# Routing tokens to experts: places counted one group later, five row buffers, a written-out group loop, and one expert tile fewer

## The reference, cut to what matters

```python
xn = layernorm(x)
h  = tanh(mean_by_dst(xn[src]) @ W1_l.T + xn @ W1_r.T + b1)
g  = mean_by_dst(h[src]) @ W2_l.T + h @ W2_r.T + b2
x2 = x + g + linear_attention(xn)          # 8 heads, q/k feature maps elu(..)+1
xf = layernorm(x2)
logits = xf @ Wr + br                       # 8 experts
e, gate = top_1(softmax over the one kept)  # gate is exp(0)/exp(0)
out = x2 + gate * (relu(xf @ W1[e] + b1[e]) @ W2[e] + b2[e])
```

## Time and profile before

| | |
|---|---|
| median of 3 runs | 2648.65 us (2645.68 to 2650.23) |
| profiled execution | 2644.86 us, its span 2642.9 us |
| TensorE busy over the span | 2436.1 us (92%) |
| VectorE, ScalarE, GpSimd busy | 1777.5, 1116.8, 1186.0 us |
| TensorE clock granted, mean | 0.967 of full |
| DMA | 511.55 MB, mean 194 GB/s |
| routing, table and empty rows, expert tiles | from about 2126, 2356 and 2374 us of the span |

### The profile page before, as it was taken

One profiled execution on the slowest core, in us unless ns is written; L12 is line 12 of the kernel. 1 busy time (PEld: TensorE's weight loads), 2 busy tenths in 40 slices (PEclk: granted clock), 3 DMA queues, 4 the chain that ended last, 5 costly groups with the idle time before them and its releaser, 6 DMA issues.

```text
span 2642.9 us, 39517 instructions
## 1 busy us (share of the span) xinstructions
PE 2436.1 (92%) x11512; PEld 1931.0 (73%) x11513; DVE 1777.5 (67%) x3701; ACT 1116.8 (42%) x2055; POOL 1186.0 (45%) x1092
## 2 busy tenths in 40 slices
PE   5999999999999998999999899899999957759897
PEld 4788888888888886888888566677777745547675
DVE  5677777767877763444344477788878567747887
ACT  3455455444444443444334323233333245535554
POOL 5576777666666660000000045555555435542333
PEclk8999999999999999999999999999999979879999
DMA  9866656455555545544444467788888687745554
GB/s 371 250 174 187 195 159 190 120 151 142 125 149 129 140 115 185 224 170 168 188 191 176 153 190 212 219 233 240 228 226 237 157 345 292 280 144 185 182 180 140
DMA packets 159400, 511.55 MB, mean 194 GB/s; under 512 B 30354, under 2 KB 30866, under 8 KB 126658
## 3 DMA queue, kind: packets, MB, share of 16 engines
q1 hardware_dynamic: 110020, 381.71, 40.8%
q0 software_dynamic: 49280, 128.61, 22.1%
HBM read 268.06 MB, written 244.32 MB: 194 GB/s over the span
## 4 chain that ended last, share of the span: by engine, by line
PE 80%; DMA 8%; DVE 5%; issue 3%; POOL 2%; ACT 1%; SPq 1%; DVEq 0%; POOLq 0%; ACTq 0%
PE bank L1363 53%; PE bank L1414 8%; PE bank L1370 5%; DMA agg_d<-O,eidx 4%; PE bank L1614 4%; PE bank L1478 2%; PE bank L1547 1%; PE bank L453 1%; PE bank L454 1%; PE bank L1617 1%; POOL r_rows L809 1%; DMA a_x<-in_x 1%; DVE r_rows L1227 1%; DVE pd L1192 1%; DVE st L1230 1%
## 5 line engine op out<-in xcount | busy, mean ns | idle before, releaser
L414 POOL DMA_INDIRECT agg_d<-O,eidx x160 | 274.4, 1715 | 221.2 <-DMA agg_d<-O,eidx 163.2
L350 POOL TENSOR_TENSOR G_low<-G,G_high 128x512 fp32r<-128x512 f32 x160 | 237.9, 1487 | 227.9 <-ACT G_high L475 227.5
L397 POOL DMA_INDIRECT G<-y_d,esrc x80 | 85.2, 1065 | 527.2 <-DMA y_d<-b_y 514.3
L433 DVE SCALAR_TENSOR_TENSOR Sj<-erow,dstf,tri 128x128 f32<-128x128 int32 x160 | 190.1, 1188 | 30.7 <-DMA agg_d<-O,eidx 30.6
L475 ACT CAST G_high<-G 128x512 fp32r<-128x512 f32 x160 | 99.2, 620 | 180.7 <-DVE G L1077 172.8
L820 POOL DMA_INDIRECT out<-x_out,x_id x88 | 84.4, 959 | 188.8 <-DVE x_out L1318 184.7
L442 DVE SCALAR_TENSOR_TENSOR eidx<-cnt,todump,dstf 128x1 int32<-128x1 f32 x160 | 149.1, 932 | 7.6
L948 ACT CAST qz_high<-low 128x512 fp32r<-128x512 f32 x80 | 49.6, 620 | 235.2 <-PE bank L1363 135.6
L774 POOL TENSOR_TENSOR pd<-pd,low 128x512 f32<-128x512 f32 (+1 forms) x80 | 142.1, 1776 | 0.0
L350 POOL TENSOR_TENSOR a_xn_rows_low<-a_x,a_xn_rows_high 128x512 fp32r<-128x512 f32 x80 | 141.6, 1771 | 0.3 <-ACT a_xn_rows_high L846 0.3
L1363 PE MATMUL bank<-Wk_high,xnT_high 128*128 128x512 f32 x320 | 127.8, 399 | 6.3 <-DVE xnT_low L350 6.3
(11 more groups left out here) (227 smaller groups left out, 7512.9 us busy)
## 6 DMA issues: line engine op xcount, KB each, us to landing
x_rows<-xs_d SPq DMA_DIRECT2D x88, 260.0 KB, 2.7
agg_d<-zero SPq DMA_DIRECT2D x20, 1040.0 KB, 20.2
b_agg<-agg_d SPq DMA_DIRECT2D x20, 1040.0 KB, 8.8
a_x<-in_x SPq DMA_DIRECT2D x20, 1024.0 KB, 7.3
agg_d<-z_halves SPq DMA_DIRECT2D x20, 1024.0 KB, 5.9
q_d<-q_rows SPq DMA_DIRECT2D x80, 256.0 KB, 2.4
r_d<-r_rows SPq DMA_DIRECT2D x80, 256.0 KB, 3.8
r_in<-r_d SPq DMA_DIRECT2D x20, 1024.0 KB, 6.8
```

Source lines behind the costliest of these rows:

```text
L350: return eng.tensor_tensor(out_, full, high.bitcast(F32), ALU.subtract)
L397: pool.indirect_dma_start(G[:, j, :], None, table, bass.IndirectOffsetOnAxis(ap=esrc[:, b, j:j + 1], axis=0)).then_inc(e_g[j], 16)
L414: pool.indirect_dma_start(agg, bass.IndirectOffsetOnAxis(ap=eidx[:, j, 0:1], axis=0), O[:, j, 0:width], None, compute_op=ALU.add).then_inc ...
L433: dve.scalar_tensor_tensor(Sj[:, :], row, dstf[:, b, j:j + 1], tri[:, :], ALU.is_equal, ALU.mult, accum_out=cnt[:, j:j + 1]).then_inc(e_cn ...
```

## The change

- `places()` is done one step later, for group g-3 at the start of VectorE's step g. VectorE's order becomes places, x2(0), x2(1), x2(2), best, x2(3). The scatter of GpSimd keeps its step.
- TensorE's `rank()` stands behind `logits(1)` instead of ahead of it.
- `r_rows`, the places and the scatter semaphores get five buffers (`RING`). The fifth takes the room of `r_part` buffer 1, which moves to the tile `G` of the edge stage, and of the copied logits, which move to `low`. SyncE waits for the last reader of `G`.
- `group_steps` writes all steps out on all five engines: no hardware loop, and waits on constants.
- The empty rows are loaded once into SBUF (`x_pad`, at step 17) and written from there.
- The 2 MB load of `W1x` moves from SyncE's step 3 to step 17. VectorE's copy into `W1x` (L1284 before) moves to the end of the table.
- `XT` is 87: the 8 experts can leave at most 8 x 127 rows unfilled, so 87 tiles hold all rows.

Cut to its core:

```diff
-XT = NT + EXP
+XT = (NP + EXP * (P - 1)) // P
+RING = 5
-def quad_turns(eng, body, tail, last=0):
-    for k in range(4):
-        body(0, k)
-    with eng.Fori(1, NG // 4 - last) as it:
-        for k in range(4):
-            body(it, k)
-...
+def group_steps(body, tail):
+    for g in range(NG + tail):
+        body(g)
...
-        rp = [at(f"r_part{i}", s, shape=[P, TG, D]) for i, s in enumerate((18, 10, 11, 14))]
+        rp = [at(f"r_part{i}", s, shape=[P, TG, D]) for i, s in ((0, 18), (2, 11), (3, 14))]
-        rows = at("r_rows", 5, shape=[P, 4, TG, AW])
+        rows = at("r_rows", 5, shape=[P, RING, TG, AW])
-        lgT = at("r_logitsT", 9.125, shape=[P, 2, GROUP])
+        pad = at("x_pad", 10.125, shape=[P, AW])
+        rp, lgT = [rp[0], G, *rp[1:]], low
...
             part_in(3, 3)
+            sp.wait_ge(e_gl, 2 * NT)
             sp.wait_ge(m_st[0], 16 * PAIRS)
...
-                if isinstance(g, int) and g == 3:
+                if g == 17:
+                    sp.dma_start(pad[:, :], pad_in).then_inc(r_pad, 16)
                     for n in range(2):
                         sp.dma_start(W1x[:, TG * D * n:TG * D * (n + 1)].bitcast(F32),
                                      f1_d[n][:]).then_inc(s_f, 16)
...
-                sp.dma_start(xs_d[bass.ds(end, P), :], pad_in).then_inc(r_pad, 16)
+                sp.dma_start(xs_d[bass.ds(end, P), :], pad[:, :]).then_inc(r_pad, 16)
...
@@ vector @@
-                        need(dve, r_sc[k], 64 * turn)
+                        need(dve, r_sc[k], 64 * (g // RING))
...
+                if g == 2:
+                    dve.wait_ge(m_st[0], 16 * PAIRS)
+                    dve.memset(rows[:, 4:RING, :, D:AW], 0.0)
+                if active(g, 3, NG):
+                    places()
                 x2(0)
                 x2(1)
+                x2(2)
                 if active(g, 2, NG):
                     best()
-                x2(2)
-                if active(g, 2, NG):
-                    places()
                 x2(3)
-            quad_turns(dve, route, 2)
+            group_steps(route, 3)
...
@@ tensor @@
                     turn_row(2)
+                    logits(1)
                 if active(g, 2, NG):
                     rank()
                 if active(g, 1, NG):
-                    logits(1)
                     turn_row(3)
```

More of the change, by code:

```diff
@@ L309, in build @@
         r_in = [sem(f"r_part_and_agg_in{k}") for k in range(4)]
-        r_sc = [sem(f"r_scattered{k}") for k in range(4)]
+        r_sc = [sem(f"r_scattered{k}") for k in range(RING)]
         r_x2 = sem("r_rdegree_x2_stats")
@@ L694, in _, with route @@
                 agg_in(k, k)
[L697 to L700, removed]
+            def route(g):
+                k = g % 4
+                if g >= 4:
+                    sp.wait_ge(r_x2, 13 * (g - 3) - 2)
                     part_in(g, k)
                     agg_in(g, k)
-                if isinstance(g, int) and g == 3:
+                if g == 17:
+                    sp.dma_start(pad[:, :], pad_in).then_inc(r_pad, 16)
                     for n in range(2):
@@ L706, in route @@
                                      f1_d[n][:]).then_inc(s_f, 16)
-                if isinstance(g, int) and g == 16:
+                if g == 16:
                     for twice in range(2):
@@ L710, in route @@
                             w2_in(W2a, twice, odd, f2_d[0])
-            quad_turns(sp, route, 0, last=1)
+            group_steps(route, 0)
+            sp.wait_ge(r_pad, 16)
             sp.wait_ge(r_tb, 1)
@@ L716, in _ @@
                 end = sp.value_load(runi[0:1, e:e + 1], min_val=0, max_val=EXP * REG - P)
-                sp.dma_start(xs_d[bass.ds(end, P), :], pad_in).then_inc(r_pad, 16)
-            for k in range(4):
-                sp.wait_ge(r_sc[k], 16 * NT // 4)
-            sp.wait_ge(r_pad, 16 * EXP)
+                sp.dma_start(xs_d[bass.ds(end, P), :], pad[:, :]).then_inc(r_pad, 16)
+            for k in range(RING):
+                sp.wait_ge(r_sc[k], 16 * NT // RING)
+            sp.wait_ge(r_pad, 16 * (EXP + 1))
             sp.wait_ge(r_tb, TB)
@@ L1199, in _ @@
             dve.tensor_copy(run[:, :], first)
-            dve.memset(rows[:, :, :, D:AW], 0.0)
+            dve.memset(rows[:, 0:4, :, D:AW], 0.0)
             dve.tensor_copy(before[:, :], cst[:, 0:P])
@@ L1536, in _, with route @@
             pe.wait_ge(m_z, NG)
-            def route(turn, k):
-                g = 4 * turn + k
+            def route(g):
+                k = g % 2
                 def logits(j):
@@ L1546, in logits @@
                     for c in range(KC):
-                        last = pe.matmul(bank[3 - k % 2][0:EXP, j * P:(j + 1) * P], wrs[:, c, :], rxT[:, j % 2, c, :],
+                        last = pe.matmul(bank[3 - k][0:EXP, j * P:(j + 1) * P], wrs[:, c, :], rxT[:, j % 2, c, :],
                                          start=c == 0, stop=c == KC - 1)
@@ L1551, in turn_logits @@
                 def turn_logits():
-                    need_apart(pe, r_lt, g - 1)
-                    need_apart(pe, r_ch, CH * (g - 4) + 3)
+                    pe.wait_ge(r_lt, g - 1)
+                    need(pe, r_ch, CH * (g - 4) + 3)
                     for j in range(TG):
-                        last = pe.transpose(bank[4 + k % 2][:, EXP * j:EXP * (j + 1)],
-                                            lgT[0:EXP, k % 2, j * P:(j + 1) * P], ident[0:EXP, 0:EXP])
+                        last = pe.transpose(bank[4 + k][:, EXP * j:EXP * (j + 1)],
+                                            lgT[0:EXP, k, j * P:(j + 1) * P], ident[0:EXP, 0:EXP])
                     last.then_inc(r_l2, 1)
```

58 lines of the change are left out of this document (27 added, 31 removed).

## The result

| | before | changed |
|---|---|---|
| median of 4 runs each | 2647.16 us (2635.09 to 2650.23) | 2615.55 us (2612.39 to 2617.31) |
| ratio | | 0.9885, 95% interval 0.9864 to 0.9906 |
| profiled execution, its span | 2644.86, 2642.9 us | 2614.40, 2612.5 us |
| first tile of routing (L1227, L1223) | 2126.39 | 2122.25 |
| last places (L1251, L1248) | 2355.11 | 2329.99 |

The change is 1.15% faster; 2625 was predicted, with a range of 2611 to 2639. The three stations cut the gain of the profiled executions, 30.4 us, into four parts. Routing, from its first tile to its last places, takes 207.7 us after 228.7: 21.0 us. From there to the first normalisation 16.7 us after 19.6: 2.9 us. The expert tiles to the end of the span 265.8 us after 268.1: 2.4 us. The other 4.1 us lie ahead of routing, in stages that the change leaves alone.

What follows compares the result with a forecast made beforehand. A chain through several engines was taken to pace routing. Gains of 17 us (routing), 3.7 (empty rows) and 2.7 (one tile) sum to 23.4: 2621.5 us for the profiled execution, a median of 2625, range 2611 to 2639.

Steps and rivals of the forecast that it cites:

- The step of 9.8 us: Routing: a new loop through VectorE, ScalarE and TensorE sets the step at 9.8 us, with about 1.2 us waiting for the rank.
- The two bounds behind it: Routing: a step can't be shorter than VectorE's own work, 8.6 us, or the round of ScalarE and TensorE, 8.8 us.
- Rival 2: Routing: the step falls to 8.8 us, what ScalarE and TensorE need; 2613 us in all, chance 0.13.
- Scatter waits gone: Routing: scatters get one more step before they are awaited, so their 7.4 us of waits are counted as gone.
- The bound of 9 us: Routing: if the two weight loads delay scatters beyond the fifth buffer's cover, at most 9 us comes back, twice the longest wait.
- The low clock: Routing: of 7.2 us put down to TensorE's lower clock, 5 us were kept in the forecast.
- rival 3: Routing: TensorE's low clock takes the stage, steps of 13.8 us; with 10 more of them 2665 us, chance 0.05.
- Last places after the places of group 17: End of routing: from the places of group 17 to the last places 15.2 us, against 16.8 before.
- Empty rows: After routing: writes from SBUF 1.10 us apart, shorter landing and the later copy gain 3.7 us, between 0.4 and 4.4.
- One tile: Expert stage: one tile fewer, bound by TensorE all through, is worth 2.7 us.
- Fetch of the written-out code: Routing: fetching the longer straight code costs nothing; a rival gave late fetching one us a step, 2648 us, chance 0.05.

Runs made afterwards that it cites:

- c2_pads_from_dram: The changed kernel with the empty rows written from DRAM again; median 2621.36 us, ratio 0.9911 to the kernel before.
- c3_tiles_88: The changed kernel with 88 expert tiles again; median 2617.02 us, ratio 0.9901 to the kernel before.

## Why the prediction was right, step by step

- **The step of 9.8 us** was 9.88, 1.1 us more over the 17 steps. Of its eight legs none is off by more than 0.06 us. That it binds is shown by cutting it: 8.66 and 8.75 us, each by moving one block of instructions. The wait for the rank, predicted as 1.2 us, is 1.21.
- **The two bounds behind it.** VectorE's 8.6 us measured 8.62 to 8.66. The round of ScalarE and TensorE, put at 8.8 as something that a step can't be shorter than, was too long: the step went down to 8.62 us. Rival 2, a step of 8.8, was no outcome of this change, and either cut gives slightly less. Its price was also off: 17 us less half is a gain of 8.5, not the 12 that the rival subtracts.
- **Scatter waits gone:** all 7.4 us. The late scatters are still there, as the four-buffer kernels show; the fifth buffer covers them. The bound of 9 us for the meeting of the weight loads was never touched; uncovered, the meeting costs 6 us in the profiles and 3 to 4 by the medians.
- **The low clock was mis-sized.** I left 5 us of it in the sum, because the new loop holds TensorE's work. None of it was left between 2160 and 2300. So the gain of the stage is 21.0 us where I had 17 and, "with no low clock left", 22. The reasons that rival 3 gave against itself are what happened: the steps got denser and the single gaps shorter, at most 1.06 us where the step of the earlier trace rows has one of 1.57 ahead of its next transposes. The order does it: 0.98 with nothing but the new order, 0.87 with everything but the order. The Trainium skill, "TensorE: Matmul & The Clock Gate", Part 1, holds that the clock is low unless activity raises it; these runs agree, 1.00 with the denser steps.
- **Last places after the places of group 17:** 15.2 us predicted, 8.75 + 6.66 = 15.4 measured.
- **Empty rows:** 3.7 us predicted, 2.9 measured, and two terms are off in opposite ways. The spacing is 1.30 us, not 1.10, and gave 1.1 us where I had counted 2.6: the register load ahead of each write (L713) has a median of 480 ns in this execution where the kernel before has 317 (L716), which I had not looked up. From the start of the last write to the tile loads it gained 1.3 us where I had 0.7, since the landing fell further, for the eight writes from a median of 3.5 us (c2_pads_from_dram) to 2.4. The copy behind the table gave the 0.4. Beside the sum I had drawn from the Trainium skill ("DMA: Bandwidth & Descriptors", Anatomy of one DMA: the target's receipt makes most of the fixed cost) that the landing gains nothing. That inference failed: same target, 1.1 us less, counted from the start of an issue that is itself 0.2 us shorter. The page's own statement, on DMAs that GpSimd issues, is not tested by these writes of SyncE.
- **One tile:** 2.7 predicted; 2.4 between the first profiles, 2.15 and 2.5 by c3_tiles_88.
- **Fetch of the written-out code:** no cost seen; the step holds no idle time of VectorE but the wait for the rank.

The sum of the parts was 23.4 us, and the parts made 26.3; 4.1 more came ahead of routing, where the start differs from run to run by more than that. 2625 stood 9.4 us above the median measured. Of that 2.9 are the parts, above all the 5 us of low clock that did not come, the term that was wrong in size, less what the longer steps, the empty rows and the tile fell short; 4.1 are the start, which was not in my sum and whose cause I can't name; and the rest is that I had put the median 3.8 us above a profiled execution, where the changed kernel's stands 1.2 above.

What made the gain, by the runs: in the routing stage the order alone gives 11.9 us of the 21.0 (16.6 against the second profile of the kernel before), and everything but the order nothing that shows beside the 4.7 us between two profiles of the kernel before. With the order in place, written-out steps give 17 x 0.3 = 5 us, and the fifth buffer the 4.1 us of the late step that is left. Over the whole kernel the parts are more even: by the medians beside each run the order alone gives 13.0 us and everything but the order 16.2, the empty rows and the tile included.

## What to carry to other kernels

When each step has the same loop through several engines, add up its legs from the start times of one step and write beside it the bound that comes next; here the next ones, two of them close together, were 1.2 us a step lower, and moving one block of code took another 20 us off the stage. A wait in the middle of an engine's step delays everybody who waits for the second half, so put it at the head, where the awaited work has had a step more. And a landing that comes 3.5 us late cost 5.5 us, one that came 2.5 late 4.1, with TensorE's clock low behind both.

## What was not expected of the hardware

- What a DMA reads from counts beside its target, by itself or by the packets that come of it: 260 KB to DRAM land in 3.5 us from DRAM (16 packets) and in 2.4 us from SBUF (128 packets), and SyncE is held for 0.54 and 0.33 us by the issue.
- TensorE held its full clock in a step of 9.88 us with gaps of 0.77, 0.29 and 1.06 us, and lost it in steps of 10.9 us with gaps of 0.77 and 2.22 us, at the same number of matmuls a step. The length of one gap doesn't decide it: in the kernel before, eight transposes took 1.97 us behind a gap of 0.88 us and 1.29 us behind one of 1.57.

```profile
2176.59 1.97 PE L1370 MATMUL bank<-ident,r_xn 128*128 128x128 f32 x8 [0.88 <-ACT r_xn L978]
...
2242.33 1.29 PE L1370 MATMUL bank<-ident,r_xn 128*128 128x128 f32 x8 [1.57 <-ACT r_xn L978]
```

- A register load from SBUF on SyncE in front of a write took from 0.26 to 0.99 us in these runs. Its median goes with the write behind it: 477 to 503 ns in the nine kernels that write the empty rows from SBUF, 275 to 410 in the five that write them from DRAM. Why is open.
